# Layer 1 of a four-layer model: the projection beside the router's softmax and search, the attention in two parts with the scatter in the first and the gathers in the second

## The reference

```python
# attention: 16 heads of 8 channels, rotary positions
q = (x @ Wq.T + bq); k = (x @ Wk.T + bk); v = (x @ Wv.T + bv)
q = q * cos + rotate_half(q) * sin            # the same for k
attn = softmax((q @ k.T) / sqrt(8)); out = (attn @ v) @ Wo.T + bo
# ffn: 32 experts, 2 of them for each token, at most 160 tokens for each expert
probs = softmax(gelu(cat(x, stats(x)) @ r1.T + b) @ r2.T)
topp, topi = top_k(probs, 2)
idx = argsort(-where(routed, probs, -inf), axis=0)[:160].T   # tokens of each expert
ye = (silu(gate) * up) @ w_down.T             # on xf[idx]; an adapter is added
out = zeros.at[idx].add(w * ye)
```

## Time and profile before

| | us |
|---|---|
| median of three runs | 2584.47 |
| profiled execution, its own time | 2584.79 |
| its span | 2583.0 |
| TensorE busy | 2021.9 (78%) |
| VectorE busy | 1799.5 (70%) |
| ScalarE busy | 1150.9 (45%) |
| GpSimd busy | 455.0 (18%) |

### The profile page before, as it was taken

The page is one execution under the profiler, slowest core; times in us unless marked ns, Lnnn a source line. Parts: engine busy times, 40 slices in busy tenths (PEclk is TensorE's granted clock), DMA queues, the critical chain, the costliest instruction groups (busy, mean ns, idle before and its releaser), DMA issues. The chain is left out here.

```text
span 2583.0 us, 45530 instructions
## 1 busy us (share of the span) xinstructions
PE 2021.9 (78%) x17632; PEld 1054.2 (41%) x17632; DVE 1799.5 (70%) x2945; ACT 1150.9 (45%) x2373; POOL 455.0 (18%) x600
## 2 busy tenths in 40 slices
PE   1787777952264969999978987997879798787898
PEld 1222222622134922333353322886534345555554
DVE  3889898766693579998835797432557698766665
ACT  1899898230001318787745222333533211156433
POOL 1111110000083122333310440113610000001100
PEclk8789899975586969999978677999989899987899
DMA  7324220000064723333200001221113424000000
GB/s 244 73 50 91 58 50 1 1 16 10 21 221 134 212 43 57 60 58 51 26 13 1 28 33 39 81 96 45 44 38 100 145 78 108 24 6 24 0 1 33
DMA packets 146771, 155.86 MB, mean 60 GB/s; under 512 B 53004, under 2 KB 122315, under 8 KB 146563
## 3 DMA queue, kind: packets, MB, share of 16 engines
q1 hardware_dynamic: 131912, 119.78, 18.0%
q0 software_dynamic: 12928, 25.47, 4.0%
q10 hardware_dynamic: 1728, 7.87, 0.7%
HBM read 87.37 MB, written 68.55 MB: 60 GB/s over the span
## 5 line engine op out<-in xcount | busy, mean ns | idle before, releaser
L419 ACT ACTIVATE a_E<-a_scores,a_nmax 128x512 f32<-128x512 f32 x512 | 343.8, 772 | 25.5 <-DVE a_nmax L354 25.0
L354 DVE TENSOR_REDUCE a_nmax<-a_scores 128x2 f32<-128x1024 f32 x256 | 303.9, 1218 | 32.3 <-PE a_scores L434 27.0
L974 ACT ACTIVATE a_E<-a_scores 128x512 f32<-128x512 f32 x512 | 271.8, 602 | 110.6 <-PE a_scores L1006 99.7
L879 DVE TENSOR_REDUCE a_nmax<-a_first 128x2 f32<-128x1024 f32 x256 | 297.5, 1218 | 28.3 <-PE a_first L996 23.8
L434 PE MATMUL a_scores<-a_Vh,a_Kh 48*128 48x512 bf16 x512 | 109.1, 424 | 109.5 <-ACT a_E L419 80.0
L447 PE MATMUL a_out<-a_E,a_QS 128*32 128x256 f32 x2048 | 174.6, 424 | 3.1 <-DVE a_QS L364 3.1
L1006 PE MATMUL a_scores<-a_Qh,a_Kh 51*128 51x512 bf16 x512 | 163.7, 392 | 14.6 <-ACT a_E L974 12.9
L996 PE MATMUL a_first<-a_Kh,a_Qh 48*128 48x512 bf16 x512 | 145.8, 417 | 23.0 <-DVE a_nmax L879 16.2
L1028 PE MATMUL a_out<-a_E,a_V 128*32 128x256 f32 x2048 | 162.0, 395 | 0.0
L419 ACT ACTIVATION_READ_ACCUMULATOR a_E<-a_scores,a_nmax 128x1 f32 x512 | 149.0, 291 | 0.0
L434 PEld LDWEIGHTS a_scores<-a_Vh,a_Kh 48*128 48x128 bf16 x512 | 25.0, 94 | 225.4 <-ACT a_E L419 176.4
(11 more groups left out here) (482 smaller groups left out, 4479.5 us busy)
## 6 DMA issues: line engine op xcount, KB each, us to landing
f_up<-in_L_up SPq DMA_DIRECT2D x32, 256.0 KB, 2.9
slots<-zeros ACTq DMA_DIRECT2D x12, 640.0 KB, 14.5
a_Kh<-a_rows_k SPq DMA_DIRECT2D x16, 384.0 KB, 6.1
a_Vh<-a_rows_v SPq DMA_DIRECT2D x16, 384.0 KB, 9.8
a_Qh<-a_rows_q SPq DMA_DIRECT2D x32, 192.0 KB, 4.6
a_Kh<-a_rows_k SPq DMA_DIRECT2D x32, 192.0 KB, 5.1
f_xe<-slots SPq DMA_DIRECT2D x40, 128.0 KB, 2.1
outs<-f_ye POOLq DMA_DIRECT2D x40, 128.0 KB
```

What stands on the lines that cost most here:

```text
L354: v.tensor_reduce(nmax[:, rd % 2, r1, :, q], bank(b, u)[:], AX.X, ALU.max, negate=True).then_inc(S["max_ready"], 1)
L419: m = a.activation(E[:, u % NE, x], bank(b, u)[:, x], ACT.Exp, bias=nmax[:, rd % 2, r1, x, q:q + 1], accum_out=Z[:, rd % 2, r1, x, q:q + 1])
L879: v.tensor_reduce(out, slot_bank(n)[:], AX.X, ALU.max, negate=True).then_inc(S["slot_read"], 1)
L974: a.activation(E[:, u % NE, x], ps_s[n % 3][:], ACT.Exp, scale=SCALE).then_inc(S["exp_ready"], 1)
```

## The change

In the router's softmax and search blocks ScalarE and GpSimd, and TensorE between its folds, now do the projection, and `project1` is gone. Its work is cut into steps (`projection1`) that these blocks call in a written order: TensorE makes one product after each fold; ScalarE adds the bias (`evict`) and does the three casts (`cast`); GpSimd does the multiplications by cos and sin (`mix`), their sum (`rotate`) and the two subtractions (`remain`), each on 128x1024 elements; VectorE only adds the bias of v (`add_v`); SP spills. The first 12 of the 40 products (`EARLY`) and 8 of GpSimd's 40 operations are in the softmax block, the rest in the search block.

```diff
+    def evict(a, b, c):
+        if b:
+            a.wait_ge(S["mixed"], 2 * b - 1 + c)
+        for h in range(2):
...
+            a.activation(F[:, c, h], ps_p[i % 4][:], ACT.Identity, bias=bqk[:, 2 * h + c:2 * h + c + 1]
+                         ).then_inc(S["evicted"], 1)
+    def mix(pool, b, c):
+        pool.wait_ge(S["evicted"], 4 * b + 2 * c + 2)
+        pool.tensor_tensor(QK[:, b % 2] if c == 0 else cross[:], F[:, c], trig[:, c].unsqueeze(1).broadcast_to([128, 2, T]),
+                           ALU.mult).then_inc(S["mixed"], 1)
+    def rotate(pool, b):
+        pool.drain()
+        pool.tensor_tensor(QK[:, b % 2], QK[:, b % 2], cross[:], ALU.add).then_inc(S["rotated"], 1)
+    def remain(pool, b, n):
+        s = b % 2
+        pool.wait_ge(S["cast"], 3 * b + n + 1)
+        pool.drain()
+        pool.tensor_tensor(both(rest[:]), both(QK[:, s] if n == 0 else rest[:]), parts[:, s, n], ALU.subtract
+                           ).then_inc(S["rested"], 1)
...
                         v.tensor_tensor(cand[:], cand[:], bits[:, i + 1:i + 2], ALU.bitwise_or)
+                        if i % 5 == 3:
+                            add_v(v, 2 + i // 5)
                         v.wait_ge(S["folded"], i + 1)
...
-                    with pe.Fori(0, 30) as i:
+                    for i in range(30):
                         pe.wait_ge(S["count_ready"], i + 1)
                         pe.matmul(ps_c[:, 0:1], fold[:], cnt[:], start=True, stop=True).then_inc(S["folded"], 1)
+                        if EARLY + i < 5 * NB:
+                            product(pe, EARLY + i)
```

```diff
+        def scatter(pool, m):
+            for t, n in pairs[per_half * m:per_half * m + per_half]:
...
+            attend1(nc, g, A, P, range(0, NB // 2), scatter, expert_ahead, None, None, None)
             g.recycle_sems()
-            experts1(nc, g, E, A["ahead"])
+            experts1(nc, g, E)
         g.recycle_sems()
-        attend1(nc, g, A, (g.outs1, idx_get, tops))
...
+        attend1(nc, g, A, P, range(NB // 2, NB), fetch, lambda sp, n: None, Y, got, tops)
```

In layer 0's attention the outputs and the projections take turns in two banks, and the table `due` is gone:

```diff
+        ps_turns = [k.ps(f"a0_turn{i}", [128, T]) for i in range(2)]
+        def out_bank(b):
+            return ps_turns[b % 2]
+        def next_bank(b):
+            return ps_turns[(b + 1) % 2]
...
                     if u in (10, 11):
                         if u == 10 and b:
-                            pe.wait_ge(S["q_read"], b)
+                            pe.wait_ge(S["added"], b)
...
-                            if u == 10 and has_prev:
-                                pe.wait_ge(S["added"], b)
-                            for n in due.get(u, (u - 8,)):
-                                outputs(b, s, n // 4, n % 4)
+                            outputs(b, s, (u - 8) // 4, u % 4)
```

More of the change, by code:

```diff
@@ L761, in unit @@
             return i, r, q
-        def batches(eng, body):
-            for b in range(NB):
-                body(b, b % 2, b > 0, b < NB - 1)
         with nc.Block() as block:
@@ L1331, in route1 @@
         SH = [128, NT, NE]
+        J = projection1(nc, g, k, weights, weights_loaded, rows)
+        product, evict, cast, mix, rotate, remain, add_v, spill, landed = (J[n] for n in (
+            "product", "evict", "cast", "mix", "rotate", "remain", "add_v", "spill", "landed"))
+        EARLY = 12
         c2 = ExitStack()
@@ L1371, in _ @@
                     a.activation(P[:], P[:], ACT.Exp).then_inc(ex, 1)
+                    a.wait_ge(weights_loaded, 4 * 16)
+                    evict(a, 0, 0)
+                    evict(a, 0, 1)
+                    evict(a, 1, 0)
+                    evict(a, 1, 1)
+                    cast(a, 0, 0)
+                    evict(a, 2, 0)
+                    cast(a, 0, 1)
+                    cast(a, 0, 2)
+                    cast(a, 1, 0)
+                @block.tensor
+                def _(pe):
+                    pe.wait_ge(weights_loaded, 4 * 16)
+                    for n in range(EARLY):
+                        product(pe, n)
+                @block.gpsimd
+                def _(pool):
+                    pool.wait_ge(weights_loaded, 4 * 16)
+                    mix(pool, 0, 0)
+                    mix(pool, 0, 1)
+                    rotate(pool, 0)
+                    mix(pool, 1, 0)
+                    remain(pool, 0, 0)
+                    mix(pool, 1, 1)
+                    remain(pool, 0, 1)
+                    rotate(pool, 1)
+                @block.sync
+                def _(sp):
+                    A["constants"](sp)
+                    spill(sp, 0)
         c3 = ExitStack()
@@ L1501, in first, with first_rows, experts1 @@
                 load_adapter(sp, e // 2)
+    def first_rows(sp):
+        rows = g.slots1.rearrange("(e p two) c -> e p two c", p=NTOK // 64 * 5 // 4, two=2)
+        for e in range(NL1):
+            sp.dma_start(E["xe"][:, e], rows[e]).then_inc(E["rows_loaded"][e], 16)
     E["load_up"], E["load_down"], E["load_adapter"], E["first"] = load_up, load_down, load_adapter, first
+    E["first_rows"] = first_rows
     return E
-def experts1(nc, g, E, ahead):
+def experts1(nc, g, E):
     NE, CAP = 32, int(1.25 * NTOK / 32)
@@ L1687 @@
+        g.sems += k.sems
 GATED_EARLY = 4
```

419 lines of the change are left out of this document (234 added, 185 removed).

## The result

The changed kernel takes 2615.27 us, median of 5 runs (2610.75 to 2623.68), against 2584.47 for the kernel before (2581.14 to 2594.8). The ratio is 1.0111 [1.0087, 1.0135]: 1.1% slower. The forecast was 2521, with a range of 2482 to 2556 and a chance of 0.03 for slower. The profiled execution took 2617.83 us and spans 2616.3.

A forecast was written before the change was run, and what follows sets the result against it. By stage: VectorE bounds softmax and search, GpSimd the projection, ScalarE layer 0's attention; TensorE nearly fills layer 1's. 2584.8 - 106.5 + 11 + 38 - 3 + 8 - 11 = 2521.3 us, range 2482 to 2556.

The forecast's parts named there:

- point 5: Layer 1's attention: splitting it in two, with scatters and gathers beside it, costs +8 us, bounds 3 and 20.
- The fourth rival: First attention part: GpSimd's maxima work queues behind ten slow scatters; 2605 us at 3.3 us a scatter; chance 4%.
- Nothing in the rows points there: First attention part: said no profile row suggests scatters slow enough to lose the gain, which takes 3.0 us each.
- Points 2 and 3: Softmax and search blocks: GpSimd holds up VectorE operations with two SBUF inputs, +11 us and +38 us.
- main case: Whole sum, 2521.3 us: GpSimd holds two-input VectorE operations but not L1411, the search's count; 66%, own range 2499 to 2545.
- The first rival: Softmax and search blocks: GpSimd holds no VectorE operation, search +0 and softmax +3, 2475 us in all; chance 17%.
- Point 6: Layer 0's attention: a round of outputs in every unit shortens ScalarE's waits for row maxima, -11 us, bounds 0 and -16.
- Points 1 and 4: Projection block disappears, -106.5 us; the experts start with first rows already loaded and TensorE coming from the attention, -3 us.

The follow-up runs named there:

- f3: Kernel before with its layer 1 gathers eight in a row in every other half, on chip 10: 2532.65 us, ratio 0.9984.
- f1: The changed kernel, unaltered, timed again on chip 10: 2467.09 us, ratio 0.973 to the kernel before.
- e8: Changed kernel with the search's two small operands, bits and clear, kept in PSUM, on chip 11: 2622.17 us, ratio 1.0092.
- g1: Changed kernel with the search's small operands in PSUM and a third buffer for v, rows of ten kept, on chip 10: 2435.56 us, ratio 0.962.
- e4: Kernel before with only layer 0's part of the change (two banks, a round of outputs in each unit): 2517.83 us, ratio 0.9917.
- e5: The changed kernel, unaltered, timed again on chip 11: 2622.81 us, ratio 1.0109 to the kernel before.
- e7: Kernel before with its layer 1 gathers ten in a row in six halves, then four, none earlier, on chip 11: 2623.28 us, ratio 1.0118.
- e6: Changed kernel with rows of eight indirect DMAs a half in place of ten, nothing spaced, on chip 11: 2619.05 us, ratio 1.0101.
- i1: Changed kernel with eight indirect DMAs a half held for TensorE's outputs, small operands in PSUM, third v buffer, on chip 13: 2527.63 us, ratio 0.9765.
- j1: Changed kernel with nine scatters or eight gathers a half, waits re-placed, small operands in PSUM, third v buffer, on chip 5: 2473.27 us, ratio 0.9567.

## Why the prediction was wrong

**The failed step is point 5**, in its sentence on the ten scatters: "10 x (1.22 + 0.30) = 15.2 us beside some 4 of its other work, in a half of 25.2". It asked whether GpSimd has the time, and it has: a scatter took 0.97 with 0.30 behind it, less than assumed. (The 25.2 is the stage over 16, its start included; the halves themselves are 21.1 and 23.1, and GpSimd's queue fits in these too.) It did not ask what the DMAs do to engines that don't wait for them. The fourth rival has the right name, the scatters hold up the first part, and the right place, but its mechanism is GpSimd's queue, which needs 3.0 us a scatter before it decides. What decided was a stall of TensorE's results that needs no slow scatter. Where nothing stalls, the attention takes 380.6 us in one part (f3) and 385.0 in two (f1), so the split with its second start is +4.4, where the forecast had +8. On the first chip the stalls are 402.9 - 380.6 = 22.3 us in the kernel before and 521.1 - 385.0 = 136.1 in the changed one. So the +118.2 are 4.4 for the split and 113.8 more of stalls, a term that the prediction did not have. The halves say the same: twelve rows of ten at 11.0 us are 132 (ten of these halves are measured whole).

**"Nothing in the rows points there" was wrong of the trace.** The kernel before has its own row of sixteen gathers in layer 2, which the prediction left out. At its end, in the kernel before:

```profile
1805.30 0.95 POOL L2162 DMA_INDIRECT f_got<-outs,f_get  x1 [0.30 <-issue]
1809.05 1.13 DVE L2261 SCALAR_TENSOR_TENSOR X<-a_ps_m,a_inv,X 128x128 f32<-128x128 f32 x4 [20.77 <-DMA f_xe<-slots]
1809.18 0.59 ACT L2216 COPY a_ypT<-a_ps_p 128x512 f32<-128x512 f32 x1 [12.18 <-DMA f_got<-outs,f_get]
1809.46 0.95 POOL L2162 DMA_INDIRECT f_got<-outs,f_get  x1 [3.21 <-DMA f_got<-outs,f_get]
...
1810.81 2.07 PE L2186 MATMUL a_ps_f<-a_ypT,a_Wfc 128*128 128x512 f32 x2 [8.95 <-ACT a_hr L2232]
```

VectorE and ScalarE come back within 0.13 us of each other though they work on different products, after 20.77 and 12.18 us, and put it down to unlike DMAs; both read a product of TensorE's. GpSimd comes back 0.3 us later, and in the code its next gather waits for TensorE (`f_done`). TensorE's 8.95 us follow from that. The groups by line say it in one row each, here of the kernel before and then of f3, on a chip without the effect:

```profile
L2186 PE MATMUL a_ps_f<-a_ypT,a_Wfc 128*128 128x512 f32 x64 | 32.5, 637 | 18.3 <-ACT a_hr L2232 18.3
```

```profile
L2186 PE MATMUL a_ps_f<-a_ypT,a_Wfc 128*128 128x512 f32 x64 | 28.8, 592 | 0.0
```

And the halves of layer 1 that the prediction took as its measure contained some 1.4 us each for their four gathers (22.3 in 16).

**The rest of the sum held.** On a chip without the effect the whole sum is close to what was measured: 2521.3 / 2584.8 = 0.9754, against 0.973 [0.9708, 0.9751] in f1. Some of that closeness is luck: between the profiles of f3 and f1 layer 0's attention gives 16 us in place of 11 and the attention costs 4.4 in place of 8, and against these the part that the change leaves alone happens to be 10 us longer in f1. Nor is it an excuse; the forecast was for the chip whose profile lay open.

*Points 2 and 3.* The operations of VectorE that were to be held are. Two rounds of the search, changed kernel, VectorE:

```profile
608.02 0.16 DVE L1522 TENSOR_SCALAR f_clear<-f_ps_c 128x1 int32<-128x1 f32 x1 [0.41 <-PE f_ps_c L1569]
608.26 2.32 DVE L1524 TENSOR_TENSOR f_cand<-f_cand,f_clear 128x1 int32<-128x1 int32 x1
610.67 1.28 DVE L1516 TENSOR_SCALAR_CACHE_REDUCE f_eqm<-f_SQ,f_cand 128x1024 f32<-128x1024 f32 x1
...
619.23 1.70 DVE L1518 TENSOR_TENSOR f_cand<-f_cand,f_bits 128x1 int32<-128x1 int32 x1
```

and GpSimd in the same stretch:

```profile
608.22 2.34 POOL L647 TENSOR_TENSOR a_cross<-a_F,a_trig 128x1024 f32<-128x1024 f32 x1 [8.22 <-ACT a_F L632]
618.80 2.12 POOL L658 TENSOR_TENSOR a_rest<-a_rest,a_parts 128x1024 f32<-128x1024 f32 x1 [8.23 <-ACT a_parts L643]
```

An operation on one element a partition, 0.16 us alone, starts 0.04 us behind GpSimd's product and ends with it, 2.32 us later; the other is held for the rest of L658. Together L1518 takes 21.5 us and L1524 18.3, where thirty rounds as in the earlier trace rows had 4.6 and 4.8: 30.4 us more. VectorE's wait for the fold gives back 10.4 of it (18.2 to 7.8). That the block came out at +37.0 against +38 is therefore in part luck: the holds cost some 20 us net and the additions for v 4, and another 12.2 are waits for v's buffer, for which the prediction has no term. L1516 stays at 1.28, as the prediction said it would in its main case. The Trainium skill, SBUF — State Buffer, section Who interferes with whom, says that a VectorE instruction with at most one SBUF input, outside the modes that use both of its port pairs, does not contend with GpSimd; e8 agrees, with 0.150 us for L1518 thirty times.

The first rival, "GpSimd holds nobody", would still have been wrong about what follows from it. With the holds gone the block was only 4 us shorter, since the wait for v's buffer in VectorE's queue grew from 12.2 us to 29.5. The two costs covered each other in part. The prediction had asked whether the additions for v fit, and not whether their buffer is free. With both taken away 110.0 us are left (g1), 35 less than in f1 and 4 more than in the kernel before. The third buffer alone was not tried.

*Point 6.* ScalarE's waits for row maxima in layer 0 went from 25.0 us, 30 times, to

```profile
ACT a_E L427 <- DVE a_nmax L360: 10.9, 9, 5.8
```

and the stage is 14.7 us shorter; the 11 were within bounds (0 and -16), and e4 shows it without the rest of the change (-13.6). *Points 1 and 4* came out within 1 us.

*The rest of the program*, which the change leaves alone, is 10.4 us shorter in the profiled execution, mostly in layer 2's scan, which ran at a granted clock of 0.93 and 0.97 in place of 0.70 and 0.83. This does not belong to the change: in e5, the same kernel, the rest takes 1257.6 us, as before the change, and in e7 1242.4. What moves the scan by some 13 us from one execution to another is open.

**What stays open.** That rows of indirect DMAs on GpSimd cause the stall is shown by e7, which has nothing else of the change; that a longer row costs more, by e6, i1 and j1, though i1 and j1 ran on chips where the changed kernel itself did not. Through what the rows reach TensorE's results is not shown: `remote` names no releaser, whether the product, its signal or its reader is late can't be told from these traces, and direct DMAs in a row, or the same DMAs from another engine, were not tried. Nor is it known what sets the chips apart; what differs is seen only in the time of the kernel before and in the stalls themselves. The best kernel measured on chips with the effect is j1's, 0.957, and on those without it g1's, 0.962; j1's was not run on the latter, nor g1's on the former. The 0.957 is both repairs together: against the changed kernel's first profile, j1's has 118 us less in the attention and 33 less in the search block.

## What to carry to other kernels

Work that one moves beside a busy engine has two prices: the time of the engine that does it, and what it does to engines that do not wait for it. For the second, look in the trace before for the same instruction in any stage, and read there whether two other engines resume at the same moment after unlike waits. On such chips put indirect DMAs of GpSimd in ones to threes between its other work, by waits on what the main engine has by then really done, and check in a timeline that they stand apart.

When one cause of a wait is taken away, ask what is next in the same queue: here holds of 30 us hid a buffer that came free late. Taking away the holds alone brought 4 us, both repairs together 35.

## What the hardware showed that I had not expected

- One program, two kinds of chip among the seven met: 2533 to 2537 us on three, 2584 to 2593 on four, for the same kernel before. For this change the sign depends on it: 1.011 and 1.011 on two of the one kind (the first and 11), 0.973 on one of the other (10). A ratio from one chip is a ratio for that chip.
- The stall grows with the row: up to three indirect DMAs in a row cost at most 1.1 us a half, ten 10.6 to 11.0, though each scatter takes the same 0.97 us on both kinds of chip, and the DMA engines are at a share of 0.04 while it lasts.
- A VectorE operation on one element a partition lasted up to 2.32 us beside a GpSimd operation, with both operands in SBUF; with one of them in PSUM it was 0.15 us every time.
